# Edge counts of a graph network: pairs of edge blocks that begin at any block, and the waits around them

## The reference

```python
dst = (3125 * uniform(key, (100000,)) ** 2.0).astype(int32)   # many edges at low targets
order = argsort(dst); src, dst = src[order], dst[order]
x = layernorm(x + edge_mlp(x, src, dst))     # L0: a two-layer network on [x[src], x[dst]], summed per target
x = layernorm(x + gcn(x, src, dst))          # L1: normalised sums over the edges, both ways
x = layernorm(x + reaction_diffusion(x, src, dst, 4))   # L2: four steps of such sums
x = layernorm(x + attention(x, src, dst))    # L3: eight heads, softmax over each target's edges
```

## Time and profile before

| | before |
|---|---|
| runs | 4036.71, 4021.42, 4037.86 us; median 4036.71 |
| the profiled execution | 4009.81 us, span 4008.1 us |
| PE busy | 3352.3 us (84%) |
| DVE busy | 2760.1 us (69%) |
| ACT busy | 1588.6 us (40%) |
| POOL busy | 1042.8 us (26%) |

### The profile page before, as it was taken

How to read it: one execution, slowest core, us unless ns; L and a number is a source line. 1 busy time by engine, 2 the same in 40 slices (tenths; PEclk the granted TensorE clock), 3 DMA queues, 4 the chain that set the end, 5 groups by cost and what they waited for, 6 DMA issues and landing times. The chain is left out here.

```text
span 4008.1 us, 83052 instructions
## 1 busy us (share of the span) xinstructions
PE 3352.3 (84%) x20322; PEld 1645.3 (41%) x20323; DVE 2760.1 (69%) x3757; ACT 1588.6 (40%) x2188; POOL 1042.8 (26%) x1056
## 2 busy tenths in 40 slices
PE   4777777678999688879989994999899989979995
PEld 2333333234444377766455552333222233332223
DVE  5988777436666466661132225999799989989995
ACT  2134566502222165541021112221588832218883
POOL 2977777755665322210000001000100000000000
PEclk9999999889999899998999997999899999989997
DMA  2255677787777587776647755111254331113343
GB/s 64 70 176 202 224 244 249 267 302 244 249 251 245 197 257 238 231 221 216 234 146 252 254 170 148 57 57 41 81 145 123 106 103 57 57 41 115 114 130 68
DMA packets 359816, 665.77 MB, mean 166 GB/s; under 512 B 134695, under 2 KB 221861, under 8 KB 358695
## 3 DMA queue, kind: packets, MB, share of 16 engines
q1 hardware_dynamic: 236288, 360.99, 28.4%
q10 hardware_dynamic: 98346, 252.14, 18.2%
q0 software_dynamic: 25088, 51.43, 4.9%
HBM read 431.49 MB, written 208.20 MB: 160 GB/s over the span
## 5 line engine op out<-in xcount | busy, mean ns | idle before, releaser
L1765 DVE SCALAR_TENSOR_TENSOR pw<-ex,c_full 128x1564 f32<-128x1564 f32 x400 | 680.8, 1782 | 35.1 <-ACT ex L1287 30.3
L1287 ACT ACTIVATE ex<-psum 128x782 f32<-128x782 f32 x800 | 610.0, 826 | 77.5 <-PE psum L2202 60.2
L841 POOL DMA_INDIRECT gat<-a_table,gidx x480 | 588.7, 1227 | 176.5 <-issue 121.7
L1727 DVE CUSTOM_DVE_ANT_0 masked<-psum,masks 128x1784 bf16<-128x1784 f32 x320 | 551.9, 1784 | 62.0 <-ACT masks L1260 43.0
L1821 PE MATMUL psum<-one_src,one_dst 128*128 x1968 | 403.9, 342 | 171.4 <-DVE one_dst L1453 99.1
L1451 DVE TENSOR_SCALAR one_src<-iota_sub,src_low 128x800 f16 x984 | 381.2, 429 | 132.5 <-PE psum L1821 70.4
L2211 PE MATMUL psum<-pw,vaug 128*32 128x391 f32 x3200 | 348.9, 508 | 29.9 <-DVE pw L1765 9.6
L1821 PEld LDWEIGHTS psum<-one_src,one_dst 128*128 x1968 | 184.3, 98 | 370.7 <-issue 286.1
L1260 ACT ACTIVATE masks<-masks,far 128x3128 bf16<-128x3128 bf16 x40 | 115.5, 2900 | 423.2 <-DMA masks<-ct_parts 423.2
L1092 ACT ACTIVATE r<-psum,vec 128x1024 f32<-128x1024 f32 x98 | 118.1, 1205 | 377.8 <-PE psum L1962 329.8
L1453 DVE SCALAR_TENSOR_TENSOR one_dst<-row_c,window_at,iota_row 128x256 f16 x492 | 234.5, 477 | 0.0
(11 more groups left out here) (350 smaller groups left out, 4893.2 us busy)
## 6 DMA issues: line engine op xcount, KB each, us to landing
c_full<-c_whole SPq DMA_DIRECT2D x80, 977.5 KB, 5.0
r_edges<-r ACTq DMA_DIRECT2D x98, 512.0 KB
r_in<-r_edges ACTq DMA_DIRECT2D x98, 512.0 KB, 3.7
c_ring<-ct_parts SPq DMA_DIRECT2D x100, 480.0 KB, 4.4
c_whole<-c_sum ACTq DMA_DIRECT2D x100, 400.0 KB
a_edges<-gat SPq DMA_DIRECT2D x148, 256.0 KB
a_in<-a_edges ACTq DMA_DIRECT2D x74, 512.0 KB, 4.4
c_ring<-ct_parts SPq DMA_DIRECT2D x100, 320.0 KB, 3.6
```

What stands on the lines that cost most here:

```text
L841: g.indirect_dma_start(to, None, a_table, bass.IndirectOffsetOnAxis(ap=rows, axis=0)).then_inc(landed, 16)
L1287: a.activation(ex[:, step_slot(n // 2), (n % 2) * 2 * CW:(n % 2 + 1) * 2 * CW].rearrange("p (h t) -> p h t", h=2), psum[:, o:o + 2 * BANK] ...
L1727: v.tensor_tensor_reduce(out=masked[:, n % 2, 0:count * width].rearrange("p (c t) -> p c t", c=count), in0=psum[:, first * BANK:(first + c ...
L1765: v.scalar_tensor_tensor(pw[:, step_slot(k), :].rearrange("p (h t) -> p h t", h=HQ), ex[:, step_slot(k), :].rearrange("p (h t) -> p h t", ...
```

## The change

The limits are found per block, not per pair: a set's run begins at its first block, wherever that is, and it takes half as many pairs as blocks, rounded up, and at least two. A run of an odd length reads one block more, which is another set's or, behind the last, an added column that matches nothing. The tables of limits have 784 entries where they had 392, in 16 bits where they had 32. `block_tab` holds a set's first block and its number of pairs.

ACT issues a set's two large transfers later: not at the end of `evict`, but in the next set's turn, behind the copy of the low part of the set before; the low part's own transfer moves behind the square.

DVE waits in the first four sets, besides for a free slot, until the pair ahead of it is made (`one_ready`).

```diff
-            pair_lim = sb("pair_lim", [WP, 2, NPAIR // WP], i32)
+            tile_lim = sb("tile_lim", [WP, 2, NT // WP], i32)
-            win = sb("win", [NWIN, 6, NPAIR], f32)
+            win = sb("win", [NWIN, 4, NT], f16)
...
             def evict(...):
                 ...
                              ).then_inc(S["evicted"], 1)
+
+            def store_window(w, q):
                 hold("act", act, S["evicted"], w + 1)
                 act.dma_start(whole_rows[ds(w * P, P), :], c_sum[:, q, :]).then_inc(c_stored[q], 16)
                 act.dma_start(count_rows[ds(w * P, P), :], c_hi[:, q, :]).then_inc(c_stored[q], 16)

-            def store_low(w, q, k):
+            def store_low(w, q, k, ahead=None):
                 act.wait_ge(S["lo_psum"], w + 1)
...
                              ).then_inc(S["lo_made"], 1)
+                if ahead is not None:
+                    store_window(*ahead)
+                after(act, S["over_ready"], w)
                 hold("act", act, S["lo_made"], w + 1)
-                act.dma_start(count_rows[ds(w * P + 4 * NP, P), :], c_lo[:, q, :]).then_inc(c_stored[q], 16)
-                after(act, S["over_ready"], w)
                 a.activation(over_out[:, :], c_lo[:, q, :], ACT.Square, accum_out=over[:, ds(w, 1)]
                              ).then_inc(S["over_ready"], 1)
+                act.dma_start(count_rows[ds(w * P + 4 * NP, P), :], c_lo[:, q, :]).then_inc(c_stored[q], 16)
...
                     if not (isinstance(w, int) and w < 2):
-                        store_low(w + -2, (m - 2) % 4, (m - 2) % SETS)
+                        store_low(w + -2, (m - 2) % 4, (m - 2) % SETS, (w + -1, (m - 1) % 4))
+                    elif w:
+                        store_window(w - 1, (m - 1) % 4)
                     evict(w, (GROUP // 4) * g + m // 4, m % 4, m % SETS)
...
+            do(v.memset(src_low[:, NT:NT + 1], 0.0))
+            do(v.memset(row_c[:, NT:NT + 1], -1.0))
...
-            do(v.tensor_scalar(win[:, 2, :], pair_bc[:, 0, :], nodeid[0:NWIN, 0:1], None, ALU.is_le))
-            do(v.tensor_scalar(win[:, 3, :], pair_bc[:, 1, :], nodeid[0:NWIN, 0:1], None, ALU.is_ge))
+            do(v.tensor_scalar(win[:, 2, :], tile_bc[:, 0, :], nodeid[0:NWIN, 0:1], None, ALU.is_le))
+            do(v.tensor_scalar(win[:, 3, :], tile_bc[:, 1, :], nodeid[0:NWIN, 0:1], None, ALU.is_ge))
             do(v.tensor_tensor(win[:, 2, :], win[:, 2, :], win[:, 3, :], ALU.mult))
...
-            do(v.tensor_reduce(out=edge_w[:, 0:2], in_=win[:, 4:6, :], op=ALU.max, axis=AX.X))
+            do(v.tensor_reduce(out=edge_w[:, 0:2], in_=win[:, 2:4, :], op=ALU.max, axis=AX.X))
...
             do(v.tensor_copy(lim_i[:, :], edge_w[:, 2:4]))
+            do(v.tensor_single_scalar(lim_i[:, 1:2], lim_i[:, 1:2], 1, op=ALU.arith_shift_right))
...
-            def one_hots(w, p, before):
+            def one_hots(w, first, p, before):
                 slot = (before + p) & (PAIRS - 1)
-                dve.wait_ge(S["slot_free"], before + p + 1)
+                at = nc.s_assert_within(dve.snap(first + p * 2), 0, NT - 1, ...)
+                if isinstance(w, int):
+                    hold("dve", dve, S["slot_free"], before + p + 1)
+                    dve.wait_ge(S["one_ready"], before + p)
+                else:
+                    dve.wait_ge(S["slot_free"], before + p + 1)
                 for t in range(2):
                     v.tensor_scalar(one_src[...], iota_sub[:, :],
-                                    src_low[:, ds(p * 2 + t, 1)], None, ALU.is_equal)
+                                    src_low[:, ds(at + t, 1)], None, ALU.is_equal)
                 v.scalar_tensor_tensor(one_dst[...],
-                                       row_c[:, ds(p * 2, 2)]...,
+                                       row_c[:, ds(at, 2)]...,
...
-                    one_hots(w, first, before)
-                    with dve.Fori(first + 1, end) as p:
-                        one_hots(w, p, before)
-                    dve.reg_add(total_dve, total_dve, end - first)
+                    one_hots(w, first, 0, before)
+                    with dve.Fori(1, length) as p:
+                        one_hots(w, first, p, before)
+                    dve.reg_add(total_dve, total_dve, length)
```

More of the change, by code:

```diff
@@ L1345, in _ @@
             for k, op in enumerate((ALU.min, ALU.max)):
[L1346 removed]
+                do(v.tensor_reduce(out=tile_lim[:, k, :], in_=edge_order[:, :].rearrange("p (g e) -> p g e", e=P),
                                    op=op, axis=AX.X))
[L1348 to L1350 removed]
+                do(v.tensor_single_scalar(tile_lim[:, k, :], tile_lim[:, k, :], 5, op=ALU.arith_shift_right))
+                do(v.tensor_reduce(out=unit_lim[:, k, :], in_=tile_lim[:, k, :].rearrange(
+                    "p (g e) -> p g e", e=UE // P),
                                    op=op, axis=AX.X))
@@ L1410, in _ @@
             dve.wait_ge(S["rows_back"], 160)
-            do(v.scalar_tensor_tensor(block_tab[:, 2, :], block_tab[:, 1, :], 512.0, block_tab[:, 0, :], ALU.mult, ALU.add))
+            do(v.scalar_tensor_tensor(block_tab[:, 2, :], block_tab[:, 1, :], 1024.0, block_tab[:, 0, :], ALU.mult, ALU.add))
             do(v.memset(lengths[:, :, :], 0))
-            do(v.tensor_tensor(lengths[:, :, :].rearrange("p t k -> p (t k)")[:, 0:NWIN], block_tab[:, 1, :],
-                               block_tab[:, 0, :], ALU.subtract))
+            do(v.tensor_copy(lengths[:, :, :].rearrange("p t k -> p (t k)")[:, 0:NWIN], block_tab[:, 1, :]))
             for k in range(1, SETS):
@@ L1445, in _ @@
             dve.sem_inc(S["one_ready"], PAIR0)
-            def one_hots(w, p, before):
+            def one_hots(w, first, p, before):
                 slot = (before + p) & (PAIRS - 1)
-                dve.wait_ge(S["slot_free"], before + p + 1)
+                at = nc.s_assert_within(dve.snap(first + p * 2), 0, NT - 1,
+                                        skip_runtime_bounds_check_because="the limits end at the tile behind the last one")
+                if isinstance(w, int):
[3 more added lines that the diff above has]
+                    dve.wait_ge(S["slot_free"], before + p + 1)
                 for t in range(2):
                     v.tensor_scalar(one_src[:, ds(slot, 1), t, 0:SUB].rearrange("p o n -> p (o n)"), iota_sub[:, :],
-                                    src_low[:, ds(p * 2 + t, 1)], None, ALU.is_equal)
+                                    src_low[:, ds(at + t, 1)], None, ALU.is_equal)
                 v.scalar_tensor_tensor(one_dst[:, ds(slot, 1), :, :].rearrange("p o t n -> p (o t) n"),
-                                       row_c[:, ds(p * 2, 2)].rearrange("p (t o) -> p t o", o=1).broadcast_to([P, 2, P]),
+                                       row_c[:, ds(at, 2)].rearrange("p (t o) -> p t o", o=1).broadcast_to([P, 2, P]),
                                        window_at[:, ds(w, 1)],
@@ L1463, in count_four @@
                 words = nc.values_load_multi_w_load_instructions(
-                    block_tab[0:1, 2, ds(4 * i, 4)], engines=[dve.engine], min_val=0, max_val=NPAIR * 512 + NPAIR)[1]
+                    block_tab[0:1, 2, ds(4 * i, 4)], engines=[dve.engine], min_val=0, max_val=NPAIR * 1024 + NT)[1]
                 for q in range(4):
-                    first = nc.s_assert_within(dve.snap(words[q] & 511), 0, NPAIR - 2)
-                    end = nc.s_assert_within(dve.snap(words[q] >> 9), 2, NPAIR)
-                    before = nc.s_assert_within(dve.snap((pairs_before(dve, total_dve) - first) & 65535), PAIR0 - NPAIR,
-                                                PAIR0 + NWIN * NPAIR)
+                    first = nc.s_assert_within(dve.snap(words[q] & 1023), 0, NT - 4)
+                    length = nc.s_assert_within(dve.snap(words[q] >> 10), 2, NPAIR)
+                    before = pairs_before(dve, total_dve)
                     w = 4 * i + q
-                    one_hots(w, first, before)
-                    with dve.Fori(first + 1, end) as p:
-                        one_hots(w, p, before)
-                    dve.reg_add(total_dve, total_dve, end - first)
+                    one_hots(w, first, 0, before)
+                    with dve.Fori(1, length) as p:
+                        one_hots(w, first, p, before)
+                    dve.reg_add(total_dve, total_dve, length)
             count_four(0)
```

38 lines of the change are left out of this document (19 added, 19 removed).

## The result

The changed kernel takes 3999.07 us (median; 3996.76 to 4008.84), beside 4031.87 us (4021.42 to 4037.86) for the kernel before: a ratio of 0.9927, interval 0.9906 to 0.9949. That is 32.8 us less; the forecast was 21.5 us less, and its range held the time. The profiled execution took 4002.94 us, span 4001.3. The one of before took 4009.8, so the two profiles differ by 7 us only.

A forecast was written before the change was run, and what follows sets the result against it. PE's own order was taken to bound the first three stretches and ACT the last forty sets; terms of 1 + 18 - 10 - 5 - 21 - 2.5 - 2 = -21.5 us took 4036.7 to 4015 us, range 3990 to 4045.

The forecast's parts named there:

- the sum: All terms added, 1 + 18 - 10 - 5 - 21 - 2.5 - 2: -21.5 us on the 4036.7 us median.
- First stage, +1: First stage: two added memsets and twice the table entries delay DVE; +1 us (+0.4 to +1.8).
- First four sets, +18: First four sets: DVE's wait makes a pair 1.42 us, so DVE binds; +18 us (-1 to +51).
- Sets 4 to 35 and 36 to 59, -10 and -5: Middle sets: ten and four pairs fewer on PE; -10 us (-12 to -5) and -5 us (-7 to -2).
- Sets 60 to 99, -21: Last sets: moved transfers shorten ACT's turn, PE's own 4.66 us a set binds next; -21 us (-24 to 0).
- GpSimd, -2: POOL's gathers: stuck until DVE's first pause, only about 11 us late by round 16; -2 us (-10 to 0).
- The rule given: Sign of being wrong: the first layer's edge stage, not edited, gets shorter by more than some us.
- The wait is not free: Rival, first four sets: the wait costs nothing and PE still binds; -40 us, 3996 us, chance 0.12.
- PE's clock did not fall: Rival, first four sets: idle PE drops to 1.2 GHz, pair 1.81 us; +12 in all, 4048 us, chance 0.14.
- The transfers came in time: Rival, last stretch: transfers land late at 278 GB/s asked, ACT waits for buffers; 0 to +2, 4037 us, chance 0.13.
- the gathers count: Rival, first layer: POOL never stuck, PE's 14.0 + 6.7 us of gather waits go; -42, 3995 us, chance 0.12.

The follow-up runs named there:

- The run with even blocks and registers: Kernel before, same pairs at even blocks, each pair's address worked out in registers from the set's first block, without run-time assertion: 4032.90 us, ratio 0.9958.
- the second profile of before: The kernel before run and profiled once more with no edit: 4044.55 us, ratio 0.9988.

## Why the prediction was right, and where it was not

The total fell inside the range, but not by the road that the sum took, and so in part by luck: up to the end of the counts stage the sum had 19.5 us and the profiles show 9. The rest, by the profiles of before, lies in the gathers, which were put at -2. By its own steps:

- **First stage, +1.** The counts began at 87.5 us for 85.6. Other profiles begin anywhere from 85.0 to 88.8 with the first stage of before and from 85.8 to 89.0 with the changed one, so the term can't be told apart. The reduction took 1.79 us, where 0.97 + 0.8 was said.
- **First four sets, +18: mis-sized, +38.** The gap was taken from a wait whose addresses were simpler, 0.27 us. That is right for the wait alone; with the registers that this change itself adds the gap is 0.42. The pair is 1.58 us, and with 82 pairs the 0.16 is 13 us of the 20 missing; 2 are the stage's later start, and the rest was not taken apart. The step named these registers, but priced them by a row that did not have them. The Trainium skill, VectorE: DVE Perf Modes, section "The DRAIN you can't avoid", measured that a semaphore after each of eight copies cost nothing. Carried over to this wait, that does not agree with the trace, where the wait leaves a gap of 0.27 or 0.42 us in each pair.
- **Sets 4 to 35 and 36 to 59, -10 and -5: -9 and -6.** The size was right, in part by luck. The run with even blocks and registers shows that it is a sum of parts I had not separated: with the registers sets 4 to 35 take 14 us more (265 for 251), and with ten pairs fewer besides they take 27 us less than that (238), more than 1.14 us a pair. How the two divide in the changed kernel stays open, since that run's work at a set's start is not quite the changed kernel's.
- **Sets 60 to 99, -21: -31.** The mechanism held, both ways round: 207 us with the holes, 188 without them and 126 pairs, 176 with 117. What failed is the next bound. I took PE's 1.03 us before a set for its own loop work, though the row itself says that VectorE's one-hot ended it. When the one-hots are there already, PE has no gap: 705.62 to 705.64 above. The 32.3 us of waits for one-hots above are what is left of it, and a set takes 176 / 40 = 4.4 us where 4.66 was taken.
- **GpSimd, -2: mis-sized.** The step reckoned that GpSimd was only 11 us late by round 16, from an execution that stuck for 67 us in all; another stuck for 84 us and more, and PE waited 45 us longer for gathers by it (51.7 for 6.7). The rule given, that I am wrong if the first layer's edge stage gets shorter, did not see it: it is 499.6 us after and 499.3 in the profile of before, but 548 in the second. I had added the distance to the median as if it lay evenly over the program.
- **The path.** The sum took every us of the counts stage for a us of the time. The profiles show that this holds only while the gathers are there in time: the edge stage ends 586 to 600 us after the counts stage, plus what PE waits for gathers. The transfers alone ended the counts stage 15 to 22 us sooner, and PE waited 46.1 us for gathers.

**The rivals.** The wait is not free. PE's clock did not fall: 0.95 was granted in the first four sets, and the pair's 1.58 us stayed under the 1.68 from which it would have decided for slower. The transfers came in time, at 259 GB/s. That the gathers count was true, but not in the rows that priced it: PE's waits for them, 14.0 + 6.7 us, are 15.1 + 7.8 after. What there is to gain stands in the second profile of before, where PE's matmuls wait 51.7 us.

**Which part did it.** Medians in us, of runs on several chips. The changed kernel and the one without the wait came back to 2 us on a second chip; the kernel before did not (4028 and 4030 on one, 4047 and 4055 on another), so differences to it are safe only beside its own run, as the ratios above have them:

| | old order | new order |
|---|---|---|
| even blocks | 4028 to 4055 | 4033 |
| even blocks, wait | 4028 | not run |
| any block | 3988 | 3965, 3967 |
| any block, wait | 4016 | 3999, 4001 |

Any block is what pays, and in two ways: fewer pairs, and an address that makes a pair 0.02 us longer, with which the gathers get through. The new order pays only on top of it, when PE's wait for gathers no longer takes it back. The wait, which pays on even blocks (4028.41 beside 4054.57 on one chip), has lost its purpose there and costs some 30 us.

## What to carry to other kernels

Before an edited stage is summed, find what the next one waits for: while that is a side engine, time gained in the edited stage is given back, and a term can be lost whole. Where the runs of a kernel spread, take one profile as one draw, and ask what in it could have gone otherwise before its stage times are used as the base. Two cures for one evil don't add: try each by itself, as here the address arithmetic freed the gathers and made the wait a mere cost.

## What the runs showed of the hardware

A gather on GpSimd stuck for 58.6 us, alike to 0.03 us in four profiles of kernels with even blocks and no wait, through 54 pairs on VectorE of 1.071 us; with pairs of 1.09 us at the median none stuck for more than 6.1 us in the counts stage, in any kernel. In neither do VectorE's rows show a pause: a pair's first one-hot starts before the last one ends, by 0.09 us there and 0.07 here. Single runs of a dozen pairs at 1.07 us occur in the free kernels too, with gathers of 3 to 6 us; the first four sets of the kernel before have runs of 57 and 65 such pairs.

The prediction had the gather go on at VectorE's first pause. In three of the four profiles it does end beside a change of set, but not in the second of before: there it ends at 88.22 + 58.58 = 146.80, and VectorE's pairs go on as they were:

```profile
145.88 0.77 DVE L1451 TENSOR_SCALAR one_src<-iota_sub,src_low 128x800 f16 x2
146.56 0.49 DVE L1453 SCALAR_TENSOR_TENSOR one_dst<-row_c,window_at,iota_row 128x256 f16 x1
146.95 0.77 DVE L1451 TENSOR_SCALAR one_src<-iota_sub,src_low 128x800 f16 x2
```

The Trainium skill, SBUF — State Buffer, section "Who interferes with whom", has the engine that issues first keep the shared port for the whole instruction, when VectorE runs in a two-port mode, and the other blocked for so long. That agrees in kind, but an instruction here is 0.4 to 0.5 us, and the wait went on through about 160 of them; whether they run in that mode no run shows. What ends the wait, and why 0.02 us a pair is enough, was not shown.
